# An expert mixture, linear attention and a quantized FFN on one core: the second layer norm in two parts, attention output from f16 parts, image 1's hidden layer during the gate

## The reference, cut to what matters

```
x = x + conv(groupnorm(x))       # 4 experts: relu(w1 xn + b1), w2 . + b2, mixed by a gate (top 2 of 4)
t = tokens(x)                    # 784 tokens of 96 channels for each image
t = t + attn(layernorm(t))       # k, v -> feature map f (t + 1 or exp t), A = f(k)' f(v) * gauss * (1 - lambda)
                                 # out = (q A) proj_w + proj_b, 12 heads of 8
t = t + ffn(layernorm(t))        # W1, W2 replaced by signs, 5 groups; both outputs scaled by the
                                 # absolute maximum of their group of 6 images; gelu between
```

## Time and profile before

| | us |
|---|---|
| median of 3 runs | 785.99 (785.55 to 786.26) |
| profiled execution | 787.79 |
| its span | 786.1 |
| TensorE (PE) busy | 736.7 (94%) |
| VectorE (DVE) busy | 671.6 (85%) |
| ScalarE (ACT) busy | 498.5 (63%) |
| GpSimd (POOL) busy | 202.7 (26%) |

### The profile page before, as it was taken

One profiled execution on the slowest core, in us unless ns is written; L12 is line 12 of the kernel. 1 busy time (PEld: TensorE's weight loads), 2 busy tenths in 40 slices (PEclk: granted clock), 3 DMA queues, 4 the chain that ended last, 5 costly groups with the idle time before them and its releaser, 6 DMA issues.

```text
span 786.1 us, 15365 instructions
## 1 busy us (share of the span) xinstructions
PE 736.7 (94%) x4811; PEld 482.4 (61%) x4811; DVE 671.6 (85%) x2001; ACT 498.5 (63%) x701; POOL 202.7 (26%) x240
## 2 busy tenths in 40 slices
PE   6699799999999999999999999999999999999991
PEld 3365456666677666677666676666776565555550
DVE  3577379999899999899998999998999678999997
ACT  1544356566666566666666565665664698988980
POOL 2352122232322233322323322323222001121110
PEclk9889999999999999999999999999999999999996
DMA  9880011111111111111111111111110102654445
GB/s 211 185 197 1 17 31 46 33 33 46 31 31 46 31 32 45 31 31 46 31 46 31 31 43 34 31 46 31 31 31 15 31 1 31 126 88 60 62 62 123
DMA packets 17773, 41.40 MB, mean 53 GB/s; under 512 B 4663, under 2 KB 4949, under 8 KB 17749
## 3 DMA queue, kind: packets, MB, share of 16 engines
q1 hardware_dynamic: 14552, 33.27, 16.4%
q0 software_dynamic: 2688, 7.23, 6.6%
q10 hardware_dynamic: 509, 0.60, 0.3%
HBM read 22.28 MB, written 18.67 MB: 52 GB/s over the span
## 4 chain that ended last, share of the span: by engine, by line
PE 63%; DVE 15%; ACT 8%; issue 6%; SPq 3%; DMA 2%; POOL 2%; DVEq 1%; ACTq 0%; POOLq 0%
PE slot L1056 15%; PE slot L1040 11%; PE slot L1267 6%; PE slot L1243 6%; PE slot L903 5%; PE slot L1062 5%; PE slot L1067 5%; DVE stage L1576 4%; PE slot L1105 4%; ACT stage L784 4%; SPq L463 3%; DVE stage L1563 1%; PE slot L1305 1%; PE slot L1301 1%; DMA big<-in_x 1%
## 5 line engine op out<-in xcount | busy, mean ns | idle before, releaser
L1056 PE MATMUL slot<-hT,w2s 128*96 128x392 f32 x384 | 138.2, 497 | 2.2 <-ACT hT L777 2.2
L1530 DVE TENSOR_SCALAR tok<-tok,ln_mv,ln_rs 112x96 f32<-112x96 f32 x434 | 109.2, 322 | 6.9 <-POOL ln_rs L609 4.4
L777 ACT ACTIVATE hT<-slot,b1c,w_unit 128x784 f32<-128x784 f32 x96 | 95.9, 1003 | 21.9 <-PE slot L1040 21.9
L609 POOL TENSOR_TENSOR ln_rs<-ln_ve,pow_half 112x7 f32<-112x7 f32 x62 | 91.8, 1481 | 4.8
L1056 PEld LDWEIGHTS slot<-hT,w2s 128*96 128x96 f32 x384 | 61.0, 165 | 49.3 <-issue 44.6
L1067 PE MATMUL slot<-big,W1b 96*128 (+1 forms) x360 | 89.2, 329 | 0.0
L839 ACT ACTIVATE hT<-slot,s 128x784 f32<-128x784 f32 x90 | 80.3, 913 | 8.1 <-DVE stage L1563 5.1
L1062 PE MATMUL slot<-big,W1b 99*128 (+1 forms) x360 | 84.4, 329 | 0.0
L1536 DVE TENSOR_REDUCE ymax<-slot 128x784 f32 (+1 forms) x90 | 83.4, 954 | 0.0
L579 POOL TENSOR_TENSOR xn_lo<-xn,xn_hi 96x784 f16<-96x784 f32 x32 | 54.4, 1699 | 109.8 <-DVE tok L1530 109.8
L606 POOL TENSOR_TENSOR ln_ve<-ln_mv,ln_eps 112x7 f32<-112x7 f32 x62 | 12.5, 202 | 269.4 <-DVE ln_mv L1524 265.9
(11 more groups left out here) (227 smaller groups left out, 1457.4 us busy)
## 6 DMA issues: line engine op xcount, KB each, us to landing
xs<-in_x SPq DMA_DIRECT2D x32, 294.0 KB, 2.8
out<-t2T SPq DMA_DIRECT2D x32, 294.0 KB, 2.6
big<-in_x SPq DMA_DIRECT2D x7, 1176.0 KB, 16.6
out<-t2T POOLq DMA_DIRECT2D x24, 294.0 KB, 4.2
big<-out SPq DMA_DIRECT2D x1, 1764.0 KB, 10.4
out<-big SPq DMA_DIRECT2D x6, 294.0 KB, 2.5
big<-in_x SPq DMA_DIRECT2D x2, 588.0 KB, 26.4
con<-shape_consts ACTq DMA_DIRECT2D x1, 445.5 KB, 6.2
```

Of the source, the lines that this page charges most:

```text
L609: nc.gpsimd.tensor_tensor(ln_rs[n][:, :], ln_ve[n][:, :], pow_half[0:TOK, 0:CHUNKS], ALU.pow).then_inc(ln_rstd[n], 1)
L777: nc.scalar.activation(hT[:, t, :].rearrange("p (a n) -> p a n", a=2), halves(t, P), ACT.Relu, scale=w1_unit[:, t:t + 1], bias=b1c[:, t:t ...
L1056: ins = mm(S[k][0:C, h, 0:HALF], w2s[:, v, t, :], hT[:, t, h * HALF:(h + 1) * HALF], start=t == 0, stop=t == TILES - 1, skip_group_check=True)
L1530: ins = V.tensor_scalar(dst[:, j, :], src[:, j, :], ln_mv[n][:, j, 0:1], ln_rs[n][:, j:j + 1], ALU.subtract, ALU.mult)
```

## The change

Three things are changed.

1. Image 1's hidden layer. Its tiles 0 and 2 are computed in step 0, in the places of the dummy matmuls, and tile 1 behind the token transposes of image 0. Their ReLU goes to a new buffer `h_second`, which later holds t2T. Step 1 starts with the mix.
2. Attention output. R is kept as two f16 parts, R_hi (a ScalarE copy) and R_lo (a VectorE subtraction, `r_low`). The output is the sum of R_hi with xh1_hi, R_hi with xh1_lo, and R_lo with xh1_hi, for each half of the image. `xh1T` and its copy are gone. So that R fits f16, a bound for it is worked out from the weights' maxima (`attention_units`) and it is scaled by a power of two, which the last step takes out again; the projection's bias becomes a row of the weights. The unit of the k and v weights, which was worked out before, moves into the same place.
3. The second layer norm. Statistics and roots are made for chunks 0 to 3 and 4 to 6 apart, each with its own semaphores; VectorE applies the first part as soon as its root is there. On GpSimd both roots now stand ahead of xn_lo.

The core of the diff:

```
...
+        FIRST_HIDDEN = [(0, 0), (0, 2), (1, 0), (0, 1), (1, 2)]
...
             def step(m, r, next_=True):                        # GpSimd
                 i = 2 * m + r
+                if not isinstance(i, int) or i >= 2:
+                    rstd(1, i - 2)
+                    rstd(2, i - 2)
                 if next_:
                     pool.wait_ge(xh1_ready, i)
                     xn_rest(1 - r, i + 1)
-                if not isinstance(i, int) or i >= 2:
-                    rstd(1, i - 2)
                 rstd(0, i)
...
-            def xh1_whole(i):                                  # ScalarE
-                act.wait_ge(xh1_lo_ready, i)
-                nc.scalar.copy(*channels(xh1T[0:C, :], 0)).then_inc(xh1T_ready, 1)
...
                     act.wait_ge(rp_ready, i)
-                    nc.scalar.copy(R[:, :], S[3][0:C + 1, 0, 0:C]).then_inc(r_ready, 1)
+                    nc.scalar.copy(R_hi[:, :], S[3][0:C + 1, 0, 0:C]).then_inc(r_hi_ready, 1)
...
+            def attention_out(done):                           # TensorE
+                def product(h, r_part, x_part, first=False, last=False):
+                    rows = C if x_part is xh1_lo else C + 1
+                    return mm(S[3][0:C, h, 0:HALF], r_part[0:rows, :], x_part[0:rows, h * HALF:(h + 1) * HALF],
+                              start=first, stop=last, skip_group_check=True)
+
+                pe.wait_ge(r_hi_ready, done)
+                product(1, R_hi, xh1_hi, first=True)
+                product(1, R_hi, xh1_lo)
+                pe.wait_ge(r_lo_ready, done)
+                product(1, R_lo, xh1_hi, last=True)
+                product(0, R_hi, xh1_hi, first=True)
+                product(0, R_hi, xh1_lo)
+                product(0, R_lo, xh1_hi, last=True).then_inc(ao_ready, 1)
...
                     pe.wait_ge(h_ready, 1)
-                    keep_busy(0, 0, 4)
+                    pe.wait_ge(xn_lo_ready, 2)
+                    hidden(0, 0, 1)
                     pe.wait_ge(seen_ready, GATES)
                     hidden(1, 1, r)
                     presences()
                     pe.wait_ge(h_ready, 2)
-                    keep_busy(0, 1, 8)
+                    hidden(2, 2, 1)
                     weights_flagged()
-                    pe.wait_ge(h_ready, 3)
+                    pe.wait_ge(h_ready, FIRST_HIDDEN.index((0, 1)) + 1)
...
+                if second:
+                    pe.wait_ge(h_ready, len(FIRST_HIDDEN))
+                    pe.wait_ge(tok1_ready, 1)
+                    mix(1, 1, 0, h_second)
...
+                if second:
+                    mix(1, 1, 2, h_second)
+                    pe.wait_ge(h_ready, len(FIRST_HIDDEN) + 1)
+                    mix(1, 1, 1, h_second, last=1).then_inc(y_mixed, 1)
...
                     to_tokens(1, t1cm[r], tok1_in_psum)
+                if first:
+                    hidden(1, 0, 1)
...
+            def attention_units():                             # VectorE, 21 instructions, ending with
...
+                link(V.tensor_scalar(r, bound, R_RANGE, 1.0 / R_RANGE, ALU.max, ALU.mult))
+                link(V.reciprocal(r_inverse, r))
+                V.tensor_copy(St[C:C + 1, C:C + 1], r_inverse[C:C + 1, :])
+                link(V.tensor_tensor(both, squared, r_inverse, ALU.mult))
+                V.tensor_scalar(gauss[:, :], con[0:C, K_GAUSS:K_GAUSS + C], lam_e[:, 2:3], both[0:C, :],
+                                ALU.mult, ALU.mult).then_inc(fold_in, 1)
...
+            def r_low(i):
+                dve.wait_ge(r_hi_ready, i)
+                V.tensor_tensor(R_lo[:, :], S[3][0:C + 1, 0, 0:C], R_hi[:, :], ALU.subtract).then_inc(r_lo_ready, 1)
...
+            def stats2(f):
+                chunk_stats(tok2, range(CH_A)).then_inc(ln_stats[1], 1)
+                chunk_stats(tok2, range(CH_A, CH_A + 1))
+                moments(1, f + 1)
+                chunk_stats(tok2, range(CH_A + 1, CHUNKS)).then_inc(ln_stats[2], 1)
+                moments(2, f + 1)
...
                 if ffn:
-                    apply(1, tok2, tok2, f, xh2_ready)
+                    apply(1, tok2, f)
+                    apply(2, tok2, f).then_inc(xh2_ready, 1)
...
                 if scales:                                     # the last attention
-                    for t in range(SPLIT):
-                        split_tile(0, 0, t)
+                    split_tile(0, 0, 0)
+                    r_low(i)
+                    split_tile(0, 0, 1)
                 if experts:
                     dve.wait_ge(tok1_ready, i + 1)
-                    stats(0, tok1, 1 if isinstance(i, int) and i == 0 else 2 * i)
+                    stats1(i)
+                if attend and not scales:
+                    r_low(i)
...
```

More of the change, by code:

```diff
@@ L268, in build @@
         Am = sb("Am", [C, C])
-        St = sb("St", [C, C + 1])
-        R = sb("R", [C + 1, C])
-        t2T = [sb(f"t2T{r}", [C, HW]) for r in range(2)]
+        St = sb("St", [C + 1, C + 1])
+        R_hi = sb("R_hi", [C + 1, C], F16)
+        R_lo = sb("R_lo", [C + 1, C], F16)
+        t2T = [h_second[0:C, r, :] for r in range(2)]
         gel = hT
@@ L787, in step @@
                 if between:
-                    for n, t in enumerate((0, 2, 1)):
-                        relu(t, n)
+                    for n, (image, t) in enumerate(FIRST_HIDDEN):
+                        relu(t, n, dst=(hT, h_second)[image])
                         if n == 0:
                             gate_exps(0, 1)
-                elif experts:
+                elif experts and not early:
                     relu(0, 0)
@@ L797, in step @@
                     tokens(tok2, 3, tok2_ready)
-                if experts and not between:
+                if experts and not between and not early:
                     relu(2, 2)
@@ L1180, in step @@
                     to_tokens(3, t2T[r], tok2_in_psum)
-                if experts and not first:
+                if experts and not first and not second:
                     wait_count(pe, ymax_done, 3 * (i - 3) + 3)
@@ L1219, in step @@
                         for t in range(TILES):
-                            mix(0, 0, t)
+                            mix(0, 0, t, h_second if second else hT)
                         pe.wait_ge(w0_copied, i + 1)
@@ L1264, in step @@
                 if attend:
-                    pe.wait_ge(r_ready, i)
-                    for h in range(2):
-                        ins = mm(S[3][0:C, h, 0:HALF], R[:, :], xh1T[:, h * HALF:(h + 1) * HALF],
-                                 start=True, stop=True, skip_group_check=True)
-                    ins.then_inc(ao_ready, 1)
+                    attention_out(i)
             mixed = None
@@ L1506, in _ @@
+            attention_units()
             dve.wait_ge(bias2_ready, 1)
@@ L1638, in step @@
                 if last:
-                    apply(0, tok1, tok1, i, xh1_ready)
+                    apply(0, tok1, i).then_inc(xh1_ready, 1)
                     absmax(f, SPLIT, SPLIT)
```

214 lines of the change are left out of this document (126 added, 88 removed).

## The result

The changed kernel took 815.69 us (median of 4 runs, 813.85 to 819.10) against 785.93: a ratio of 1.0373, 95% interval 1.0342 to 1.0404. The forecast was 780.3 with a range of 770.5 to 787, so it was wrong, in its sign too. Rival 1, which had been given a chance of 0.15, had 816.7.

What follows compares the result with a forecast made beforehand. In the loop TensorE's issue plus short stalls was taken to bound the kernel, with VectorE some 1.4 us slack per image. Head -4.0, loop -2.0, tail +0.3 gave -5.7: 780.3 us against the median, range 770.5 to 787.

Steps and rivals of the forecast that it cites:

- Rival 1: Loop, every image: GpSimd's xn_lo takes the port between the apply's parts, VectorE stands 1.5; 34.4 longer, 816.7 us; chance 0.15.
- the split in the loop: Loop, second layer norm in two parts: no cost, as xn_lo (1.67 long) waits for the seven applies' end.
- Loop: Images in the loop: period 16.61 against 16.68, 0.07 per image, 2.0 us off over 28 images.
- The lost 0.33: Loop: of the 0.40 TensorE saves per image in attention output, 0.33 is lost waiting for the third maximum.
- Head: Before the loop: 2.5 (image 1 early) + 0.6 and 0.9 (images 2 and 3) = 4.0 us shorter.
- the collision of step 2: Head: GpSimd's xn_lo of image 3 against the gate's second half on VectorE goes, 0.6 off.
- Head, the clock: Head, image 1: after standing still 2.7, TensorE may run 3.2 us at half speed again, losing 1.6.
- Head, the units: Head, VectorE before t1cm of image 0: 21 added instructions take 3.0 (2.75 to 3.6); t1cm starts 1.5 later, at 82.5.
- The scaling of gauss: Head, one VectorE instruction among those that compute the units: taken as 0.25.
- Tail: Image 32: R_lo stands behind the split of a gelu tile, so attention output ends later; 0.3 longer, nothing hides it.

## Why the prediction was wrong

**The step that failed** stands in the paragraph on the split in the loop: "The seven applies follow each other just so, so I take it that xn_lo waits for their end and costs nothing". xn_lo enters at the first change from one apply to the next. The seven took 3.21 in place of 1.76, and 17.78 - 16.64 = 1.14 of it came through in an image of the loop. I had taken the order in which L1403 and xn_lo ran for a rule, though it was one boundary between two instructions of another kind, and had given the other outcome 0.15. It was not even a rule there: in the kernel before with the split alone, the same two engines in the same step came out the other way (last section). One row showed VectorE held up, one showed it not held up, and the price of being wrong was 34 us; such a pair does not bear a range that leaves one of them out.

The Trainium skill ("SBUF — State Buffer", section "SBUF: two separate sides") gives the pair of ports to the instruction that starts first, for its whole length, and names as VectorE's users of it the instructions in a two-port mode and those with two SBUF inputs. The runs agree on the length: the apply stood until xn_lo's end. They also agree that t1cm and the feature maps, with one of their two inputs in PSUM, are no such users: they kept 1.02 and 1.74 beside it. The applies have one tensor input, and no row shows in which mode they ran; nor do the recorded starts tell who was first, as the apply that stood is recorded 0.05 ahead of xn_lo in the change. Read for each apply apart, and not for the group of seven, that rule allows rival 1.

**Rival 1** had the sign, the place and the price (816.7, period 17.91; measured 815.69 and 17.78), but not the position: it put the stall at the last applies, with xn_lo some 0.7 behind the first one's start, and it is the second, with xn_lo 0.28 behind. Of the stall of 1.46, 1.14 came through, where the rival had 1.3 of 1.5. Its sign, one apply of over 1 us in each image, is what the trace shows.

**The rest of the sum** is tested by the two kernels that differ from the change in xn_lo's place alone: 781.60 and 780.19, where the forecast was 780.3.

- *Loop.* Forecast 16.61 and 2.0 off; measured 16.64, and 1.7 off from image 3 to 31, of which 0.5 lies at the loop's entry. The lost 0.33 is shown: with the maxima's order changed the period falls by 0.31, with a second R_lo it rises by 0.13, and without R_lo the same order changes nothing. But it was not all lost before the third hidden tile, as forecast: 0.17 is wait for the first maximum and 0.12 wait at the third tile. Not foreseen was that the shorter period needs the split (16.75 in one part), which I had put at no gain in the loop.
- *Head.* Forecast 4.0 off. I count from VectorE's reduction seen_any (73.58 before, 74.72 after), since its own place lay between 69.91 and 74.72 in the traces. From there image 3's copy of R came after 66.35 before, 62.34 and 62.60 in the two kernels: 4.0 and 3.8 off, with a mean granted clock of 0.95 over the stretch in all three. The parts do not bear the sum out. Up to image 1's transposes to channels 2.4 and 1.1 were off (20.75 before, 18.36 and 19.68; forecast 2.5), from there to image 3 1.6 and 2.7 (forecast 1.5), and the 1.6 belongs to xn_lo ahead of the roots, where the collision of step 2, 0.6 of that forecast, is still there. So that the head's sum came out is in part luck.
- *Head, the clock.* The row at 0.54 behind the wait of 2.17, from which I worked, was one execution's. In three other kernels with the same code up to there (the split alone, the split with the maxima's order changed, and xn_lo behind the root) the clock was 1.00 behind that wait, the mix took 4.19 in place of 5.64, and the transposes came 19.31 after seen_any in place of 20.75. With the change's first part they came 17.52 to 20.00 after it, 17.52 at a clock of 1.00. So with the clock at 1.00 on both sides they came 1.8 earlier, by one profile of the changed code, where I had 2.5. The mix with the split alone:

```profile
86.67 4.19 PE L1059 MATMUL slot<-hT,w2s 128*96 128x392 f32 x12 [2.16 <-ACT hT L780]
```

- *Head, the units.* t1cm of image 0 came 1.77 later, not 1.5: the units took 3.54, near the upper end of 3.6. In the profile of the change it stood at 83.88, past the 83 that I had named as a sign against me. The scaling of gauss took 0.65 of it and not 0.25 (it took 0.32 before). It ended 0.07 behind an instruction of GpSimd, which fits the same hold-up, though no run tests it:

```profile
81.24 0.65 DVE L1569 TENSOR_SCALAR gauss<-con,lam_e,r_unit 96x96 f32<-96x96 f32 x1
81.27 0.55 POOL L612 TENSOR_TENSOR kvw_lo<-kvw,kvw_hi 97x192 f16<-97x192 f32 x1
```

- *The collision in step 2* is gone as forecast: L1439, the L1405 of the earlier trace rows, takes 0.21 after the change, and 0.86 again with xn_lo ahead of the roots. But it cost 0.6 once, and moving xn_lo costs 1.14 in every image.
- *Tail.* Forecast 0.3 longer, measured 0.34 in this pair of profiles. That does not show the term: from the last copy of R to the end it is 164.85 to 165.41 in the four kernels without R_lo, and 165.03 (xn_lo behind the applies) to 168.53 (xn_lo ahead of the roots, where the clock fell to a mean of 0.82 over the first 18.63) with it.

## What to carry to other kernels

Where GpSimd's work is moved, look at what kind of instruction VectorE has beside it in the new place, one by one: beside a run of short SBUF-to-SBUF instructions in float32, GpSimd can enter at the first boundary, and the next one pays for its whole length; beside the seven applies of the change it did so in most images of the loop. Put it beside VectorE work that reads PSUM, or beside statistics, where it cost nothing here. And an instruction added ahead of work that frees buffers for the busiest engine takes back what that engine saved, until that work is put ahead of it.

## What the runs showed of the hardware

VectorE and GpSimd took turns by instruction beside the applies, yet in step 2 xn_lo, recorded from 104.11 in the kernel with xn_lo ahead of the roots, let two TENSOR_TENSORs of VectorE go first and was 0.8 longer, as in the earlier trace rows:

```profile
104.11 2.49 POOL L592 TENSOR_TENSOR xn_lo<-xn,xn_hi 96x784 f16<-96x784 f32 x1 [2.55 <-DVE tok L1613]
104.38 0.38 DVE L1436 TENSOR_TENSOR stage<-stage 112x224 f32<-112x224 f32 x1
104.68 0.38 DVE L1437 TENSOR_TENSOR stage<-stage 112x224 f32<-112x224 f32 x1
105.10 0.85 DVE L1438 RECIPROCAL stage<-stage 112x112 f32<-112x112 f32 x1
105.87 0.86 DVE L1439 TENSOR_TENSOR stage<-stage 112x112 f32<-112x112 f32 x1
```

It is not that TENSOR_TENSORs keep GpSimd out. In the kernel before with the split alone the first of the same two stood, for 1.46 (1.84 in place of 0.38):

```profile
105.11 1.86 POOL L580 TENSOR_TENSOR xn_lo<-xn,xn_hi 96x784 f16<-96x784 f32 x1 [2.30 <-DVE tok L1545]
105.38 1.84 DVE L1405 TENSOR_TENSOR stage<-stage 112x224 f32<-112x224 f32 x1
107.15 0.38 DVE L1406 TENSOR_TENSOR stage<-stage 112x224 f32<-112x224 f32 x1
```

In both traces xn_lo is recorded 0.27 ahead of the first of the two. With the split undone (1.65) and with the split and the maxima's order changed (1.83) it was the first that stood as well. So of five traces in which the two engines met there, GpSimd came in at the first boundary in three and behind the second in two. What decides it stays open.

The granted clock behind the same wait of TensorE (2.65 to 2.75, for t1cm of image 0) was not the same from one execution to the next. Two windows from there to image 1's transposes, in the kernel with xn_lo behind the applies and in the one with the first maximum ahead of R_lo:

```profile
82.00:90.50 8.50, 8.50 (x26) 4.30 (x25) 3.56 (x21) 4.13 (x6) 3.31 (x3) 0.69 0.11 34
```

```profile
82.00:88.50 6.50, 5.96 (x23) 2.79 (x20) 3.56 (x21) 4.14 (x6) 1.73 (x2) 1.00 0.17 46
```

The mean is 0.69 in one (part of the stretch at 1.2 GHz) and 1.00 (2.4 GHz) in the other, and the transposes came 19.68 and 17.52 after seen_any. A single profile of such a stretch is good to some 2 us, which is nearly as much as the 2.5 that I had for image 1.
